# PE takes a group's sums behind the fetch of its first chunks in the attention layers of a graph network

## The reference

```
xw    = x @ W                           # per head ch values: 64 in layer 1, 32 in layer 2
xi,xj = xw[dst], xw[src]
alpha = (sum(xj*att_l) + sum(xi*att_r)) * sigmoid(sum(xi*xj))
alpha = where(alpha > 0, alpha, 0.2*alpha)
e     = exp(alpha - segment_max(alpha, dst)[dst])
out   = segment_sum(xj * e, dst) / (segment_sum(e, dst) + 1e-16) + bias
```

## Time and profile before

| | |
|---|---|
| median of 3 runs | 6434.16 us |
| the profiled execution | 6430.39 us |
| its span, first to last instruction | 6428.8 us |
| busy share PE, PEld, DVE, ACT, POOL | 66%, 46%, 59%, 19%, 56% |
| mean granted PE clock over the span | 0.837 |
| gathers of both edge passes (line 1027) | 1742.1 to 4334.0 us |

### The profile page before, as it was taken

One profiled execution on the slowest core, in us unless ns is written; L12 is line 12 of the kernel. 1 busy time (PEld: TensorE's weight loads), 2 busy tenths in 40 slices (PEclk: granted clock), 3 DMA queues, 4 the chain that ended last, 5 costly groups with the idle time before them and its releaser, 6 DMA issues. The chain is left out here.

```text
span 6428.8 us, 102457 instructions
## 1 busy us (share of the span) xinstructions
PE 4263.4 (66%) x26702; PEld 2979.1 (46%) x26703; DVE 3787.8 (59%) x8560; ACT 1190.0 (19%) x1987; POOL 3580.3 (56%) x3658
## 2 busy tenths in 40 slices
PE   0666667395267777776256666663777778777884
PEld 0111114263156565665245566652555456565663
DVE  8777772154589898898556666665111235555553
ACT  0111111012211111111211221121211222222221
POOL 1222224502377777774277777770666667777772
PEclk9999999698589999998567676676888888889886
DMA  4000004200244444444233333335222222222233
GB/s 192 12 15 14 12 15 182 63 21 30 72 127 116 124 117 124 123 116 83 78 81 81 80 81 80 79 67 180 60 63 61 66 69 78 78 78 78 78 78 42
DMA packets 332968, 513.66 MB, mean 80 GB/s; under 512 B 104565, under 2 KB 245919, under 8 KB 322966
## 3 DMA queue, kind: packets, MB, share of 16 engines
q0 software_dynamic: 130656, 290.33, 17.9%
q1 hardware_dynamic: 202166, 221.78, 10.7%
HBM read 409.97 MB, written 101.86 MB: 80 GB/s over the span
## 5 line engine op out<-in xcount | busy, mean ns | idle before, releaser
L1027 POOL DMA_INDIRECT e_ring<-att_rows,e_near x1792 | 1845.3, 1030 | 550.5 <-issue 483.6
L1094 PE MATMUL e_psum<-e_ring,e_whole_pick 128*128 128x264 f32 (+1 forms) x3584 | 864.5, 395 | 303.8 <-DVE e_ring L1254 293.8
L1784 POOL DMA_INDIRECT e_nodes<-x,e_edges x832 | 807.4, 970 | 266.0 <-issue 242.6
L1094 PEld LDWEIGHTS e_psum<-e_ring,e_whole_pick 128*128 128x128 f32 x3584 | 664.2, 230 | 430.7 <-issue 204.2
L1049 PE MATMUL e_px<-t_parts,e_pick 128*128 x5376 | 694.9, 271 | 111.1 <-DVE e_pick L1156 51.8
L1172 DVE TENSOR_TENSOR e_prod<-e_px,e_ring 128x512 f32<-128x512 f32 x672 | 458.1, 682 | 492.5 <-DMA e_ring<-att_rows,e_near 411.6
L285 PE MATMUL b_acc<-b_pick_key,b_pick_lo 128*128 128x416 bf16 (+1 forms) x1960 | 496.7, 340 | 169.5 <-DVE b_pick_key L256 151.1
L1049 PEld LDWEIGHTS e_px<-t_parts,e_pick 128*128 128x128 bf16 x5376 | 455.8, 108 | 204.2 <-issue 134.5
L1701 POOL DMA_INDIRECT sorted<-rx_held,rx_index x432 | 426.4, 987 | 221.8 <-issue 212.1
L355 PE MATMUL r_pa<-gru_counts,gru_parts 128*128 x3000 | 452.0, 317 | 135.5 <-DMA r_bh<-in_gru_bh 117.7
L1136 ACT ACTIVATE e_whole_pick<-e_pturn 128x512 f32<-128x512 bf16 x448 | 266.4, 595 | 1318.0 <-PE e_pturn L1085 1294.3
(11 more groups left out here) (336 smaller groups left out, 6294.3 us busy)
## 6 DMA issues: line engine op xcount, KB each, us to landing
e_relb<-place SPq DMA_DIRECT2D x56, 1024.0 KB
e_ring<-att_rows,e_near POOLq DMA_INDIRECT x1792
sorted<-o_fill SPq DMA_DIRECT2D x11, 2508.0 KB
e_edges<-sorted SPq DMA_DIRECT2D x209, 132.0 KB
kept<-gin_counts SPq DMA_DIRECT2D x5, 4000.0 KB, 35.3
gru_counts<-kept SPq DMA_DIRECT2D x5, 4000.0 KB
rx_held<-in_edge_rows POOLq DMA_DIRECT2D x52, 297.0 KB
e_nodes<-x,e_edges POOLq DMA_INDIRECT x832
```

The source lines that it names most:

```text
L1027: pool.indirect_dma_start(out=ring[:, s, r, 0:wd + HEADS], out_offset=None, in_=xrows, in_offset=bass.IndirectOffsetOnAxis(ap=near[:, s, r ...
L1094: mm = pe.matmul(psum[q % 2][:, 0:RING], whole_pick[:, q % 2, c, :], ring[:, s, q * G + c, :], start=(c == 0), stop=(c == G - 1))
L1784: pool.indirect_dma_start(out=nodes[:, q, u, :], out_offset=None, in_=source, in_offset=bass.IndirectOffsetOnAxis(ap=edges[:, q, u, RBF + ...
```

## The change

In `step` of PE the call of `apply` moves from the end of the place to a point behind the first fetch (and the even chain step). The new order is: fetch part 0; chain step 2i; apply; turn_pick of the next group; fetch part 1; chain step 2i+1. No instruction is added or taken away, and no wait is changed.

```
@@ -1104,6 +1104,9 @@  (step, in the block of the tensor engine)
                         fetch(k, s, i, 0, t)
                     if maxima and 2 * i in chain:
                         chain[2 * i](k)
+                    now = summing(k, s, i, prev, cur)
+                    if now:
+                        apply(*now)
                     nxt = following(k, s, i, prev, cur)
                     if nxt:
                         turn_pick(*nxt)
@@ -1111,9 +1114,6 @@
                         fetch(k, s, i, 1, t)
                     if maxima and 2 * i + 1 in chain:
                         chain[2 * i + 1](k)
-                    now = summing(k, s, i, prev, cur)
-                    if now:
-                        apply(*now)
```

## The result

The changed kernel takes 7082.81 us, the median of 4 runs (7077.33 to 7088.63), against 6435.24 us for the kernel before in the same session (4 runs): a ratio of 1.1005, 95% interval 1.0986 to 1.1024. Forecast were 7025 us, 6740 to 7250. The profiled execution took 7088.63 us, its span is 7087.0 us, with a mean granted clock of 0.817.

The account below looks back on a forecast made before the run. POOL's gathers were taken to pace both edge passes before the change. Forecast: 6430.4 + 575 (layer 1) + 0 (layer 2) + 16 (ends) = 7021 us profiled, 7025 us as median, range 6740 to 7250.

Parts of the forecast that it names:

- The bound and the loop: Layer 1: POOL's pace gives way to scale, sums, fetch part 1, second score_rows, next scale; 7.02 us a place, +298 us.
- the two halves of the rule: PE's queue: a partial reorder window lets fetch part 1 pass waiting sums (6434 us), or matmuls keep program order.
- Layer 1's own time: DVE's time for a layer 1 block without stalls: 36.67 us for places 0 to 6, some 4.4 for place 7; 41.1 us.
- The stalls: Layer 1: DVE waits before second score_rows, 15.0 us a block at full clock; with 58% low clock, +575 us in all.
- Layer 2: Layer 2's edge pass: new waits stay hidden beneath POOL's gathers, so 0 us; 117 us if that fails.
- The cover that POOL's pace gives: Layer 2: POOL's pace hides turn_pick and chain steps behind the sums, at worst 4.4 us a block.
- The ends: Last 12 places of both passes: copy and signals lie between sums, 1.0 us in eight places of each layer, 16 us.
- A: Rival: PE's clock stays up in layer 1's loop; 6748 us, chance 0.14.
- B: Rival: PE's clock stays down throughout, layer 1's loop 9.62 us long; 7300 us, chance 0.11.
- C: Rival: as forecast, but in layer 2 POOL's pace fails to hide the new waits, 117 us more; 7142 us, chance 0.06.
- E: Rival: nothing changes, as PE works past the waiting sums or stalls fit beneath POOL's pace; 6434 us, chance 0.04.
- D: Rival: earlier sums free ring rows, gathers start earlier, DVE waits less; at most 62 us gained, 6372 us, chance 0.03.

Follow-up runs that it names:

- early_scale: The changed kernel with DVE's scale of the next place's group moved one place ahead, behind the first score_rows; 7442.5 us, 1.0099 of the kernel before beside it.
- early_both: The changed kernel with DVE's scale one place ahead and its add moved from the place's end to its start; 7375.9 us, 1.0010 of the kernel before.
- fetches_first: The changed kernel with fetch part 1 ahead of the sums: both fetches, sums, then transposes; 7325.0 us, 0.9948 of the kernel before beside it.
- warm36: The changed kernel with 36 unread 128-column matmuls before the sums in layer 1's 212 places; 7612.2 us, 1.0339 of the kernel before beside it.

## Why the prediction was right

**The bound and the loop.** Right in kind and in size. DVE's second score_rows at full clock starts at T + 4.50, as the sum of rows had it, and early_scale, early_both and fetches_first each open the loop at another place, with layer 1's places coming back to 1507, 1413 and 1352 us from 1822 (the old order has 1363). Only the last opens it fully.

**PE's order.** PE starts no matmul past the waiting sums: in the timeline above it stands idle for 2.86 us ahead of them, and fetch part 1, whose inputs were there, starts only behind them. The idle time lies ahead of the sums in all of the 212 places. Of the two halves of the rule weighed in the prediction (the Trainium skill, "TensorE: Matmul & The Clock Gate", "Part 3: Packing small matmuls") the trace bears out the one by which matmuls keep the program's order. The prediction took the same from the earlier trace rows, and that row doesn't show it: the next place's fetch needs the bank that DVE's first score_rows still reads, and in the kernel before this ran until 2220.24, when the sums had started at 2219.89:

```profile
2219.57 0.67 DVE L1172 TENSOR_TENSOR e_prod<-e_px,e_ring 128x512 f32<-128x512 f32 x1
```

So the conclusion was right, on a row that couldn't carry it.

**Layer 1's own time.** 41.1 us a block were forecast, 42.5 measured (1822.5 less the 695 us that DVE stands before second score_rows, over 26.5 blocks). This is +38 us. Of these 27 are pauses ahead of `scale` at the turn of the loop, put down to issue, 11 of them; the first line of the earlier trace rows has one of 2.02 us, and the block was counted from behind it. The other 11 were not taken apart.

**The stalls.** 15.04 us a block at full clock are 399 us; the trace has 695 us, so the clock adds 296 us. Forecast were 277, by way of a wrong middle: 0.71 was taken for the granted clock and 0.78 measured, so less of the time is spent at the low level, but more of the places are hit. 153 of 212 have score_rows at T + 6 or later (to the nearest half), not half of them, and each for 1.9 us on average instead of 2.6. Of the 153 falls of the clock in this stretch 93 come while PE is idle and 60 in the sums just behind the gap, and the clock comes back during the work that follows. So the low level lies on the loop: of the 957 us between the sums and second score_rows 656 are at 1.2 GHz, of the 546.5 us of PE's gap ahead of the sums only 106. The two errors nearly cancel: the mechanism was right, but that the size of this term came out within 20 us is luck.

**Layer 2.** 0 forecast, -11.6 measured. POOL's gathers are that much shorter (973 to 960 ns each, 11.6 us in all) and its idle time is the same; why they are shorter is open. The cover that POOL's pace gives held.

**The ends.** 16 us forecast, 33 measured. In layer 1 the mechanism is right (2.95 instead of 2.06 us from sum to sum). Layer 2's end was not read at all but given layer 1's 1.0 us in eight places; it takes 20.4, and most of what was missing is the clock. The sum prices the low level for the loop and not for the ends, and here the clock stays low behind the new waits (0.54 where it was 0.86), so that the sums themselves take 2.18 instead of 1.17 us. It is so in every kernel with the transposes behind layer 2's sums: clock 0.54 to 0.65 in this end and 42 to 46 us, against 0.72 to 0.87 and 26 to 31 us with the transposes ahead of them.

Together: +38 and +19 for layer 1, +17 for the ends, -12 for layer 2 make 62 of the 67 us between the 7021 forecast for a profiled execution and the 7088.6 measured. Of the rest 2.6 us are the window of the earlier trace rows, which reaches past the last score_rows, so that 1189.8 us were taken where 1187.2 belong.

**The rivals.** A, the clock up throughout, gives 6748 us; it is out at a granted clock of 0.78, and warm36 shows that the clock stays up (0.94) only when PE is given work. B is out by the same 0.78. C is out, as layer 2 got shorter, and E by the 648 us. D's mechanism shows in layer 2 in the second session (-66 us in its places, +19 in its end), and not in the first.

## What to carry to other kernels

On an engine that takes its work in order, a wait belongs behind everything that others wait for and that doesn't need it. Before a wait is moved up, list what gets queued behind it, and follow that to see if it leads back to who ends the wait: if so, the place is as long as the whole ring, however much room each engine has. And where such a ring leaves gaps on PE, price its part at both clock levels, with the low one on the part behind the gap, and do the same for the ends of the pass.

## What was not expected of the hardware

- The same kernel took 6435 us in one session and 7364 to 7367 us on three chips in a later one. First scale in layer 1 starts at 1809 us in the one and at 1861 to 1865 in the other, and the stretch that PE and DVE bound took 1822 us in both, at nearly the same granted clock (0.78 and 0.79). So these engines were as fast; whether the chip or something else in the session slows the rest was not separated.
- With PE idle for 2.6 us on average ahead of the sums (mostly 2.3 to 3.2), in places of 6.5 to 9 us, 153 of 212 places had their second score_rows some 1.5 us or more later than at full clock; 18 added matmuls of 128 columns in each place (about 1 us) brought the mean granted clock from 0.79 to 0.90.
- In layer 2's end the changed kernel's PE was busy for 32.4 of 46.0 us and idle for 0.69 us ahead of each sum, and its granted clock was still only 0.54. A low clock doesn't need long gaps there; what decides it was not found out.
